# Final LayerNorm of a decoder block: roots of three quarters by VectorE, two quarters stored ahead of the last reload

## The reference

```python
x = _layernorm(x + attention(x))                  # 16 heads
x = _layernorm(x + cross_attention(x, ctx_1024))  # softmax over the heads
x = _layernorm(x + ffn(x))                        # one shared expert, 15 routed ones

# ffn
weights = softmax(x @ gW + gb)                    # 15 experts
topv, topi = top_k(weights, 3)
y = shared_expert(x) + sum(topv[k] * expert[topi[k]](x) for k in range(3)) + x

# _layernorm, eps = 1e-05
(x - mean(x)) / sqrt(var(x) + eps)
```

## Time and profile before

| | |
|---|---|
| median of 3 runs | 285.23 us (285.05 to 285.29) |
| the profiled execution | 285.98 us |
| its span (first to last instruction) | 284.1 us |
| PE busy | 230.8 us (81%) |
| DVE busy | 220.7 us (78%) |
| ACT busy | 190.7 us (67%) |
| POOL busy | 183.3 us (65%) |
| DMA | 31.90 MB, mean 112 GB/s |

### The profile page before, as it was taken

One profiled execution on the slowest core, in us unless ns is written; L12 is line 12 of the kernel. 1 busy time (PEld: TensorE's weight loads), 2 busy tenths in 40 slices (PEclk: granted clock), 3 DMA queues, 4 the chain that ended last, 5 costly groups with the idle time before them and its releaser, 6 DMA issues.

```text
span 284.1 us, 7099 instructions
## 1 busy us (share of the span) xinstructions
PE 230.8 (81%) x2283; PEld 175.7 (62%) x2283; DVE 220.7 (78%) x613; ACT 190.7 (67%) x420; POOL 183.3 (65%) x170
## 2 busy tenths in 40 slices
PE   7988999887799788659957889975898996989840
PEld 3777777675554344334524466665698996978830
DVE  7775999997999999999995579724164673878784
ACT  4597998754798589767645755425177784777663
POOL 7043474443047584589896877777767777777874
PEclk9999999998999979988989799999599998999995
DMA  6694471012500000049603115351424437375464
GB/s 184 248 254 93 87 220 42 6 38 75 150 0 2 0 0 2 14 115 367 227 30 121 47 52 146 102 127 57 115 68 123 115 94 220 104 214 139 155 198 139
DMA packets 38597, 31.90 MB, mean 112 GB/s; under 512 B 12864, under 2 KB 31552, under 8 KB 38432
## 3 DMA queue, kind: packets, MB, share of 16 engines
q1 hardware_dynamic: 34608, 23.90, 30.0%
q0 software_dynamic: 3520, 7.27, 7.5%
q10 hardware_dynamic: 432, 0.27, 0.3%
HBM read 19.95 MB, written 11.47 MB: 111 GB/s over the span
## 4 chain that ended last, share of the span: by engine, by line
DVE 36%; PE 23%; issue 16%; POOL 11%; DMA 8%; ACT 3%; SPq 2%; DVEq 1%; POOLq 0%; ACTq 0%
POOL x_srt L1954 9%; DVE prob_sums L1493 7%; PE psum L983 5%; DVE maxes L1487 5%; DMA k_heads<-x_srt 5%; PE psum L992 4%; PE psum L569 3%; DVE prob_sums L1407 2%; PE psum L620 2%; PE psum L975 2%; PE psum L586 1%; DVE maxes L1402 1%; DVE v_rows L1478 1%; SPq L458 1%; DMA xT<-x_t 1%
## 5 line engine op out<-in xcount | busy, mean ns | idle before, releaser
L2016 POOL DMA_INDIRECT y_tok<-k_heads,y_rows x62 | 61.6, 994 | 19.9 <-issue 14.5
L1311 ACT ACTIVATE k_heads<-psum,k_heads 128x128 f32<-128x128 f32 x124 | 38.7, 363 | 35.5 <-PE psum L983 30.6
L1954 POOL DMA_INDIRECT x_srt<-v_blocks,slot x48 | 47.2, 983 | 15.4 <-issue 15.1
L1931 POOL TENSOR_TENSOR k_heads<-k_heads,inv_sums 128x1024 f32<-128x1024 f32 x16 | 30.9, 1939 | 25.2 <-DVE inv_sums L1498 25.1
L983 PE MATMUL psum<-k_heads 128*128 128x128 f32 x248 | 40.2, 286 | 3.7 <-DVE k_heads L1810 3.7
L1810 DVE COPY k_heads<-psum 128x128 f32<-128x128 f32 x62 | 17.9, 288 | 31.1 <-PE psum L975 30.0
L992 PE MATMUL psum<-k_heads 128*128 128x128 f32 x248 | 39.1, 281 | 0.3 <-ACT k_heads L1311 0.3
L983 PEld LDWEIGHTS psum<-k_heads 128*128 128x128 f32 x248 | 33.8, 198 | 5.2 <-DVE k_heads L1810 4.7
L1919 POOL TENSOR_TENSOR probs<-probs,inv_sums 128x512 f32<-128x512 f32 x16 | 16.7, 1048 | 28.3 <-DVE inv_sums L1412 28.1
L992 PEld LDWEIGHTS psum<-k_heads 128*128 128x128 f32 x248 | 33.9, 198 | 0.5 <-ACT k_heads L1311 0.5
L1794 DVE COPY k_heads<-expert_w 128x514 f32 x62 | 27.2, 444 | 3.4 <-issue 2.6
(11 more groups left out here) (189 smaller groups left out, 524.3 us busy)
## 6 DMA issues: line engine op xcount, KB each, us to landing
expert_w<-e_w SPq DMA_DIRECT2D x1, 4369.0 KB, 16.0
k_heads<-x_srt SPq DMA_DIRECT2D x62, 65.0 KB
q_heads<-y_tok SPq DMA_DIRECT2D x8, 256.0 KB, 3.5
x_srt<-pad SPq DMA_DIRECT2D x16, 65.0 KB
xT<-x_t SPq DMA_DIRECT2D x4, 256.0 KB, 5.8
ctxT_k<-ctx_k SPq DMA_DIRECT2D x2, 512.0 KB, 5.5
v_scr<-v_rows SPq DMA_DIRECT2D x4, 256.0 KB, 2.8
ctxT_v<-ctx_v SPq DMA_DIRECT2D x2, 512.0 KB, 5.4
```

The lines of the kernel that those rows point to most:

```text
L1311: ins = act.activation(h_tile[:, t % 2, a, :], bank[2 + t % 2][:, P * a:P * a + P], ACT.Gelu, bias=tile_weights(t)[:, EW - 2 + a:EW - 1 + a])
L1931: pool.tensor_tensor(probs2[:, p % 3, :].rearrange("p (t h) -> p t h", t=B), probs2[:, p % 3, :].rearrange("p (t h) -> p t h", t=B), inv_s ...
L1954: pool.indirect_dma_start(out=x_srt, out_offset=bass.IndirectOffsetOnAxis(ap=slot[:, n:n + 1], axis=0), in_=payloads[:, g, k, :], in_offse ...
L2016: pool.indirect_dma_start(out=y_tok, out_offset=bass.IndirectOffsetOnAxis(ap=y_rows[:, t:t + 1].bitcast(mybir.dt.uint32), axis=0), in_=y_t ...
```

## The change

- VectorE computes the roots of quarters 0, 1 and 2 by itself. `root_seed` makes a first value from the bit pattern of var + eps (two instructions: a shift, then a product with -1 and a sum with 0x5f3759df), and `root_newton` is one Newton step of three instructions, done three times. Quarters 0 and 1 are done together (eight values in a row) between the tiles 52 to 54; quarter 2 behind the tiles.
- GpSimd's two `pow` go, and so do quarter 2's reciprocal and its `Sqrt` on ScalarE. Only quarter 3 has a `Sqrt`.
- VectorE normalises quarter 0 in tile 55. ScalarE normalises quarter 1, two groups in each of its steps 56 and 57, between tiles.
- SP stores the eight groups of quarters 0 and 1 ahead of the last reload instead of behind it.

```diff
@@ -355,7 +354,7 @@
         RELOAD_LAG = 9
         RELOAD_LAST = 57
         SUMS_AT = (39, 48, 57)
-        ROOTS_AFTER = 53
+        ROOTS_AT = 52
         SHARED_TILES = (8, 14, 20, 26)
         SHARED_BANK = (6, 6, 5, 4)
 
...
@@ -491,17 +487,20 @@
                     for k in range(NB):
                         sp.wait_ge(s_y_scattered[k], landed[k])
                     reload_y(sp, NC - 2)
+            for g in range(4):
+                sp.wait_ge(s_final_v, g + 1)
+                store(sp, 0, g)
+            for g in range(4):
+                sp.wait_ge(s_final, g + 1)
+                store(sp, 1, g)
             for k in range(NB):
                 sp.wait_ge(s_y_scattered[k], landed_all[k])
             reload_y(sp, NC - 1)
-            for g in range(4 * (NC - 2)):
-                sp.wait_ge(s_final_v, g + 1)
-                store(sp, g // 4, g % 4)
             for g in range(4):
-                sp.wait_ge(s_final, g + 1)
+                sp.wait_ge(s_final, 5 + g)
                 store(sp, NC - 2, g)
             for g in range(2):
-                sp.wait_ge(s_final_v, 4 * (NC - 2) + 1 + g)
+                sp.wait_ge(s_final_v, 5 + g)
                 store(sp, NC - 1, g)
             sp.wait_ge(s_out, 16 * NC * PAIRS)
 
...
@@ -1297,9 +1296,15 @@
             shared_gelu(6)
             shared_gelu(7)
 
-            def root3(c0, c1):
-                act.wait_ge(s_ln3, ln3_steps(c1))
-                act.activation(rstd3[:, 4 * c0:4 * c1], rstd3[:, 4 * c0:4 * c1], ACT.Sqrt).then_inc(s_rstd3, 1)
+            def applied3(first, count, half):
+                act.wait_ge(s_nmean3, half)
+                for g in range(first, first + count):
+                    act.activation(acc[:, g, :], acc[:, g, :], ACT.Identity, bias=nmean3[:, g:g + 1],
+                                   scale=rstd3[:, g:g + 1]).then_inc(s_final, 1)
+
+            def root3():
+                act.wait_ge(s_ln3, 2 * NC + 1)
+                act.activation(rstd3[:, 4 * (NC - 1):NG], rstd3[:, 4 * (NC - 1):NG], ACT.Sqrt).then_inc(s_rstd3, 1)
 
             for i in range(NT + 1):
                 if i < NT:
...
@@ -1318,20 +1323,14 @@
                         act.wait_ge(s_y_scattered[t % NB], 16 * (t // NB))
                     act.activation(y_tile[:, t % NB, :], bank[6 + t % 2][:, 0:E], ACT.Copy,
                                    scale=x_tile[:, t % NB, E:E + 1]).then_inc(s_y_tile, 1)
-
-
-            def applied3(first, count, half):
-                act.wait_ge(s_nmean3, half)
-                for g in range(first, first + count):
-                    act.activation(acc[:, g, :], acc[:, g, :], ACT.Identity, bias=nmean3[:, g:g + 1],
-                                   scale=rstd3[:, g:g + 1]).then_inc(s_final, 1)
-
-            root3(NC - 2, NC - 1)
+                if i in (ROOTS_AT + 4, ROOTS_AT + 5):
+                    applied3(4 + 2 * (i - ROOTS_AT - 4), 2, 1)
+
             applied3(4 * (NC - 2), 4, 2)
-            root3(NC - 1, NC)
+            root3()
             applied3(NG - 2, 2, 3)
             for g in range(2):
-                act.wait_ge(s_final, 5 + g)
+                act.wait_ge(s_final, 9 + g)
                 store(act, NC - 1, 2 + g)
 
 
...
@@ -1844,20 +1843,29 @@
                 for j in range(4):
                     ins = dve.bn_aggr(mean_var3[:, 4 * c + j, :], bn3[:, 4 * c + j, :])
                 ins.then_inc(s_ln3, 1)
-                dve.wait_ge(s_ln3, ln3_steps(c) + 1)
+                dve.wait_ge(s_ln3, 2 * c + 1)
                 dve.tensor_scalar(var_eps3[:, 4 * c:4 * c + 4], mean_var3[:, 4 * c:4 * c + 4, 1], EPS, None, ALU.add).then_inc(s_ln3, 1)
-                if c >= NC - 2:
-                    dve.wait_ge(s_ln3, ln3_steps(c) + 2)
+                if c == NC - 1:
+                    dve.wait_ge(s_ln3, 2 * c + 2)
                     dve.reciprocal(rstd3[:, 4 * c:4 * c + 4], var_eps3[:, 4 * c:4 * c + 4]).then_inc(s_ln3, 1)
 
-            def sum_mean(c0, c1, root):
+            def root_seed(c0, c1):
                 gs = slice(4 * c0, 4 * c1)
-                dve.wait_ge(s_rstd3, root)
+                dve.wait_ge(s_ln3, 2 * c1)
+                routed(dve.tensor_scalar(rstd3[:, gs].bitcast(I32), var_eps3[:, gs].bitcast(I32), 1, None, ALU.logical_shift_right))
+                routed(dve.tensor_scalar(rstd3[:, gs].bitcast(I32), rstd3[:, gs].bitcast(I32), -1.0, float(0x5f3759df),
+                                         ALU.mult, ALU.add))
+
+            def root_newton(c0, c1):
+                gs = slice(4 * c0, 4 * c1)
                 routed(dve.scalar_tensor_tensor(out=newton3[:, gs], in0=var_eps3[:, gs], scalar=-0.5, in1=rstd3[:, gs],
                                                 op0=ALU.mult, op1=ALU.mult))
                 routed(dve.tensor_tensor(newton3[:, gs], newton3[:, gs], rstd3[:, gs], ALU.mult))
                 routed(dve.scalar_tensor_tensor(out=rstd3[:, gs], in0=newton3[:, gs], scalar=1.5, in1=rstd3[:, gs],
                                                 op0=ALU.add, op1=ALU.mult))
+
+            def sum_mean(c0, c1):
+                gs = slice(4 * c0, 4 * c1)
                 dve.scalar_tensor_tensor(out=nmean3[:, gs], in0=mean_var3[:, gs, 0], scalar=-1.0,
                                          in1=rstd3[:, gs], op0=ALU.mult, op1=ALU.mult).then_inc(s_nmean3, 1)
 
...
@@ -1879,6 +1887,16 @@
                     shared_result(NC - 1)
                 if t % 4 == 1:
                     tile_rows(t - 1)
+                if t == ROOTS_AT:
+                    root_seed(0, NC - 2)
+                    root_newton(0, NC - 2)
+                if t == ROOTS_AT + 1:
+                    root_newton(0, NC - 2)
+                if t == ROOTS_AT + 2:
+                    root_newton(0, NC - 2)
+                    sum_mean(0, NC - 2)
+                if t == ROOTS_AT + 3:
+                    sum_applied(0, 4, 1)
                 for c in range(NC - 1):
                     if t - SUMS_AT[c] in (0, 1, 2):
                         added(c, t - SUMS_AT[c])
...
@@ -1888,17 +1906,17 @@
                     expert_of = expert_staged(t + 2, expert_of)
 
 
-            dve.wait_ge(s_rstd3_early, NC - 2)
-            gs = slice(0, 4 * (NC - 2))
-            dve.scalar_tensor_tensor(out=nmean3[:, gs], in0=mean_var3[:, gs, 0], scalar=-1.0, in1=rstd3[:, gs],
-                                     op0=ALU.mult, op1=ALU.mult).then_inc(s_nmean3, 1)
-            sum_applied(0, 4 * (NC - 2), 1)
+            root_seed(NC - 2, NC - 1)
+            for n in range(3):
+                root_newton(NC - 2, NC - 1)
+            sum_mean(NC - 2, NC - 1)
             added(NC - 1, 0)
             added(NC - 1, 1)
-            sum_mean(NC - 2, NC - 1, 1)
             added(NC - 1, 2)
             sum_stats(NC - 1)
-            sum_mean(NC - 1, NC, 2)
+            dve.wait_ge(s_rstd3, 1)
+            root_newton(NC - 1, NC)
+            sum_mean(NC - 1, NC)
             sum_applied(4 * (NC - 1), 2, 3)
 
 
...
@@ -2016,11 +2034,6 @@
                 pool.indirect_dma_start(out=y_tok, out_offset=bass.IndirectOffsetOnAxis(
                     ap=y_rows[:, t:t + 1].bitcast(mybir.dt.uint32), axis=0),
                     in_=y_tile[:, t % NB, :], in_offset=None).then_inc(s_y_scattered[t % NB], 16)
-                if t == ROOTS_AFTER:
-                    for c in range(NC - 2):
-                        pool.wait_ge(s_ln3, ln3_steps(c + 1))
-                        pool.tensor_tensor(rstd3[:, 4 * c:4 * c + 4], var_eps3[:, 4 * c:4 * c + 4], minus_half[:, :],
-                                           ALU.pow).then_inc(s_rstd3_early, 1)
             pool.wait_ge(s_scattered, 16 * (SOON - 1))
             pool.wait_ge(s_late_rows, 16 * (1 + TOPK * NG - SOON))
             for k in range(NB):
```

More of the change, by code:

```diff
@@ L310, in build @@
         s_rstd3 = sem("s_rstd3")
-        s_rstd3_early = sem("s_rstd3_early")
         s_final = sem("s_final")
@@ L366, in reload_y @@
                                 ).then_inc(s_y_loaded[c] if c < NC - 1 else s_y_last[k], 16)
-        def ln3_steps(c):
-            return 2 * min(c, NC - 2) + 3 * max(c - (NC - 2), 0)
         def tile_of(m, what):
```

## The result

| | before | changed |
|---|---|---|
| median of 16 runs each | 285.47 us | 287.07 us |
| ratio | 1 | 1.0052 (95%: 1.0029 to 1.0075) |
| the profiled execution, its span | 285.98, 284.1 us | 285.25, 283.5 us |
| VectorE's copy of tile 52 | 260.03 us | 258.20 us |
| from there to the end of the span | 24.07 us | 25.30 us |

A ratio leaves out the executions that lie more than 1.5% above the quickest of their kernel, while medians and means take all, so the two can stand apart.

What follows compares the result with a forecast made beforehand. VectorE's last addition of quarter 3 sets the end; VectorE alone would start it 0.35 us earlier, but the reload behind eight stores makes it +0.2 us: 285.23 + 0.2 = 285.4 us, range 284.5 to 286.5.

Steps and rivals of the forecast that it cites:

- VectorE's path behind the tiles: From the last `tile_rows` to the last addition: 4.05 us instead of 4.91; with quarter 2's reciprocal gone, -0.95 us.
- VectorE's path in the tiles: Work added ahead of tile 57's addition: 3.6 us, of which 3.1 is covered; 0.6 us late with the stagings.
- The start of the reload: SP issues the last reload behind eight stores, at 271.6 instead of 269.76, 1.85 us later.
- The landing of the third reload DMA: Issued at 272.45, landing at 276.85 with the median of 4.4 us; the last addition at about 276.9 waits for it.
- The last stores: Stores at the kernel's end may land faster; bounds 0 and -0.3 us, taken as 0.
- The sum: Change of +0.2 us: profiled execution 286.2 us, median 285.23 + 0.2 = 285.4 us.
- Rival 2: Reload queues behind the stores' data and lands 0.65 to 1.3 us later: +0.8 to +1.45, 286.3 us; chance 0.20.
- both of its signs: DMA share 0.4 or more in the 2 us ahead of the reload; over 5 us from third issue to addition.
- Rivals 1 and 3: 1: VectorE stays the bound, 284.6 to 284.9 us, chance 0.27; 3: ScalarE's table load late, 285.6 us, chance 0.05.

Runs made afterwards that it cites:

- half_first: Changed kernel with quarter 0's four stores ahead of the last reload and quarter 1's four behind it; 0.9988 of the kernel before in the first job.
- reload_first: Changed kernel with the last reload issued ahead of all eight stores, run twice (_2 is the second); 0.9979 and 1.0005 of the kernel before.
- waits_only: Changed kernel with SP's waits for the eight normalised groups kept ahead of the reload, the stores behind it; 0.9977 and 1.0011 of the kernel before.

## Why the prediction was wrong

- **VectorE's path behind the tiles: right.** 4.05 us were worked out; in half_first it took 274.51 - 270.36 = 4.15, from the last `tile_rows` to the last addition.
- **VectorE's path in the tiles: right.** 0.6 late forecast, 0.7 measured. Together VectorE alone was to be 0.35 earlier at the last addition; reload_first_2 shows 16.67 - 16.31 = 0.36.
- **The start of the reload: right.** Forecast 271.6, which is 11.57 behind tile 52's copy; measured 11.70 to 11.75, in three profiles. The waits_only runs show that ScalarE's four normalisations make 0.9 us of the two, and the stores behind them the other 1.1.
- **The landing of the third reload DMA: the step that failed.** "With the median of 4.4 it lands at 276.85." Measured were 5.5, 5.1 and 4.7 us, 5.1 in the mean, issued at 12.56 to 12.81 where 12.42 was forecast. That is 0.7 + 0.25 = 0.95 us, and the mean of the last addition, 17.80, is 0.93 behind the forecast 16.87. The median was that of four reloads; the row also had this reload's own value, 4.8, which the same text used to say when the data had come before. With 4.8 the forecast would have been +0.6. Against 4.8, the 5.1 of the changed kernel is no clear lengthening, given 4.7 to 5.5 in three profiles. The second DMA was given no landing of its own; at 5.1 us it held the last addition in the first profile just as long as the third. The first took 3.7 to 3.9 where 3.4 was used, and VectorE waited 0.5 to 0.8 us for it.
- **The last stores: right within its bounds.** From the last addition to the end 7.40 us before, 7.14 to 7.22 after.
- **The sum.** The mean end of the three profiles is 24.97, so +0.9 us; the executions say +1.1 (+1.5 in the first 16). The rest of 0.2 is within their errors. Of the time itself, 0.24 us is the base: the forecast started from a median of three, 285.23, and that of 16 is 285.47.
- **Rival 2** had the size (+0.8 to +1.45; the additions show +0.9 to +1.4) and both of its signs (the second one in two of three profiles: 5.5, 5.1 and 4.8 us), but, as far as the runs show, not its cause: with no store ahead of the reload the third DMA took 5.2 and 5.1 us (waits_only), with eight right ahead and no scatters 4.3. Its signs did not tell its cause from a landing that is long by itself. The scatters beside it lengthen the landing, by 0.4 us in one pair of profiles. Why the landing was 5.5 in one profile and 4.7 in another of the same kernel stays open. GpSimd's pause for its two roots, costed at nothing, was not tried by itself, nor were stores right behind the reload.
- **Rivals 1 and 3** fall: the reload never started before 271.1 (11.1 behind tile 52's copy), and the table load had 2.6 us to spare.

No version was shown to beat the kernel before at 285 us: reload_first and half_first end 0.1 to 0.55 us earlier in their profiles, which their executions can't tell from no change.

## What to carry to other kernels

A queue that issues in order makes each DMA wait for everything that those ahead of it wait for. Ahead of a load that the end depends on may stand only stores whose data is ready before the load's own condition: four stores that were cost nothing, four that weren't cost more than the roots had gained. And where a forecast turns on a landing, take that transfer's own time from the trace, not a median over calmer ones, and count from an event close by when whole executions scatter by more than 1%.

## What was not expected of the hardware

- The same instructions ahead of the change reached tile 52 at 257.6 to 261.7 us in the ten profiles of the table: more spread than any effect studied here.
- Two of four jobs ran every kernel 14% slower. The VectorE and ScalarE instructions took the same time (0.68 us for an addition, 1.28 for the table load). TensorE's busy time rose from 230.8 to 243.4 us of a span of 284.1 and 321.9, and its granted clock was 0.92 where it had been 0.94; the rest is idle time, part of it on TensorE without a wait that the profile shows:

```profile
L992 PE MATMUL psum<-k_heads 128*128 128x128 f32 x248 | 41.5, 291 | 14.7 <-issue 8.2
```

This is the kernel before in the second job; at 284 us the same line had 0.3 us idle. The cause of the slower jobs stays open.
- Reload DMAs of the same size took 3.3 to 5.5 us from issue to landing at the same place of the program.
